# Cross attention of the last two sequences, started four rounds later

## What is computed

```python
x = _layernorm(x + _L0_attn_ref(...))
x = _layernorm(x + _L0_xattn_ref(...))
x = _layernorm(x + _L0_ffn_ref(...))
x = _layernorm(x + _L1_attn_ref(...))    # stage D: linear attention, 16 heads, causal
x = _layernorm(x + _L1_xattn_ref(...))   # stage E: cross attention, 16 heads, softmax
x = _layernorm(x + _L1_ffn_ref(...))     # stage F: 8 experts, the best two of each token
```

```python
attn = einsum('bhqd,bhkd->bhqk', q, k) * scale
attn = softmax(clip(attn, -CLAMP, CLAMP))
x = einsum('bhqk,bhkd->bqhd', attn, v).reshape(B, Nq, Cq) @ Wo + bo
```

## Time and profile before

| | |
|---|---|
| median of 3 runs | 1518.58 us (1508.76 to 1525.29) |
| profiled execution | 1518.51 us, its span 1516.7 us |
| PE, DVE, ACT, POOL busy | 1328.6, 908.3, 575.2, 801.0 us |
| mean granted clock of PE | 0.924 |
| PE waits of scores for the queries' load, 1018 to 1130 us | 19.4 us, 2 times |
| DVE busy, 1059.3 to 1080.2 and 1080.2 to 1109.7 us | 16.00 and 16.85 us |
| first expert block's transposes on PE | from 1198.51 us |

### The profile page before, as it was taken

The page is one execution under the profiler, slowest core; times in us unless marked ns, Lnnn a source line. Parts: engine busy times, 40 slices in busy tenths (PEclk is TensorE's granted clock), DMA queues, the critical chain, the costliest instruction groups (busy, mean ns, idle before and its releaser), DMA issues.

```text
span 1516.7 us, 23092 instructions
## 1 busy us (share of the span) xinstructions
PE 1328.6 (88%) x9071; PEld 1131.0 (75%) x9071; DVE 908.3 (60%) x1729; ACT 575.2 (38%) x1171; POOL 801.0 (53%) x762
## 2 busy tenths in 40 slices
PE   6996999999999999978898988986865399999990
PEld 6995788888888888855576666765754399999990
DVE  4666522732442452234577777786774499999986
ACT  3566211211111121023244444443432377777752
POOL 4433666666666576323123334334533678888742
PEclk9997899999999999988799999998776599999995
DMA  5100333333233233112233124224210666656615
GB/s 172 38 17 6 101 97 118 97 98 97 83 103 95 81 111 97 35 51 55 75 117 112 44 94 112 49 88 124 84 35 15 227 229 237 222 216 226 218 60 166
DMA packets 58044, 163.23 MB, mean 108 GB/s; under 512 B 10598, under 2 KB 26185, under 8 KB 50000
## 3 DMA queue, kind: packets, MB, share of 16 engines
q1 hardware_dynamic: 45760, 100.13, 22.4%
q0 software_dynamic: 12176, 61.63, 11.4%
HBM read 136.47 MB, written 27.08 MB: 108 GB/s over the span
## 4 chain that ended last, share of the span: by engine, by line
PE 70%; DVE 14%; DMA 5%; ACT 4%; issue 3%; SPq 2%; POOL 1%; another core or an unknown queue 0%; ACTq 0%; POOLq 0%; DVEq 0%
PE bank L386 16%; PE bank L388 15%; PE bank L387 15%; PE bank L1214 8%; PE bank L394 5%; PE bank L975 3%; PE bank L1056 2%; DVE topE L1717 2%; DVE shiftE L1726 2%; SPq L715 2%; DMA split_qk<-qk_lo 2%; DMA xt_hi<-split_qk 1%; PE bank L1132 1%; PE bank L1043 1%; ACT x_tok L434 1%
## 5 line engine op out<-in xcount | busy, mean ns | idle before, releaser
L1590 DVE CAST hid_hi<-bank 128x512 fp32r<-128x512 f32 x96 | 66.4, 692 | 252.0 <-ACT bank L1329 250.9
L518 POOL TENSOR_TENSOR wpiece_lo<-wraw,wpiece_hi 128x1024 fp32r<-128x1024 f32 x88 | 210.9, 2397 | 7.4
L387 PE MATMUL bank<-hid_lo,wpiece_hi 128*128 128x512 f32 x512 | 199.4, 390 | 0.0
L386 PE MATMUL bank<-hid_hi,wpiece_lo 128*128 128x512 f32 x512 | 199.4, 389 | 0.0
L388 PE MATMUL bank<-hid_hi,wpiece_hi 128*128 128x512 f32 x512 | 199.4, 389 | 0.0
L516 POOL TENSOR_SCALAR wpiece_hi<-wraw 128x1024 fp32r<-128x1024 f32 x88 | 93.9, 1067 | 157.4 <-PE bank L388 129.5
L1329 ACT ACTIVATE bank<-bank,ffn_scales 128x512 f32<-128x512 f32 x64 | 42.4, 662 | 301.5 <-PE bank L388 301.5
L634 POOL TENSOR_SCALAR staging<-staging 128x1024 f32<-128x1024 f32 x64 | 66.6, 1041 | 134.3 <-ACT staging L1414 134.0
L1414 ACT ACTIVATE staging<-bank 128x512 f32<-128x512 f32 x128 | 70.0, 596 | 119.7 <-PE bank L1132 77.2
L386 PEld LDWEIGHTS bank<-hid_hi,wpiece_lo 128*128 128x128 f32 x512 | 96.2, 188 | 20.1
L388 PEld LDWEIGHTS bank<-hid_hi,wpiece_hi 128*128 128x128 f32 x512 | 96.1, 188 | 20.0
(11 more groups left out here) (337 smaller groups left out, 3752.2 us busy)
## 6 DMA issues: line engine op xcount, KB each, us to landing
wraw<-in_C_w SPq DMA_DIRECT2D x88, 512.0 KB, 3.6
split_qk<-qk_hi SPq DMA_DIRECT2D x64, 128.0 KB, 2.4
split_qk<-qk_lo SPq DMA_DIRECT2D x64, 128.0 KB, 2.4
xt_lo<-split_qk SPq DMA_DIRECT2D x8, 1024.0 KB, 5.7
xt_hi<-split_qk SPq DMA_DIRECT2D x8, 1024.0 KB, 5.8
yc<-y_rows SPq DMA_DIRECT2D x16, 256.0 KB, 5.8
ctx_raw<-in_ctxT SPq DMA_DIRECT2D x16, 192.0 KB, 4.0
xraw<-in_xT SPq DMA_DIRECT2D x8, 256.0 KB, 3.8
```

What stands on the lines that cost most here:

```text
L386: pe.e.matmul(o, sl, mh, start=start and i == 0, stop=False)
L387: pe.e.matmul(o, sh, ml, start=False, stop=False)
L518: pool.e.tensor_tensor(pair[1], raw, f(pair[0]), ALU.subtract).then_inc(done, 1)
```

## The change

For the last two sequences e becomes d + 22, so their PAIR, EDR and EFIN steps stand four rounds later; EPRE, which was written from e, is written from d and stays where it was.

```diff
         d = 4 + PAIRS * b
-        e = d + 18
+        e = d + (18 if b < B - 2 else 22)
...
-        items.append((e - 6, 5, "EPRE", (b,), (0, 1, 2, 7)))
+        items.append((d + 12, 5, "EPRE", (b,), (0, 1, 2, 7)))
         items += [(e + p, (0, 1, 2), "PAIR", (b, p), (0, 2, 4)) for p in range(PAIRS)]
         items += [(e + 8 + 4 * c, 5, "EDR", (b, c), 1) for c in range(KC)]
         items.append((e + 13, 5, "EFIN", (b,), (0, 1, 2, 4, 4, 5, 7, 8)))
```

## The result

The changed kernel took 1504.76 us (median of 19 runs, 1495.25 to 1519.68), the kernel before 1519.49 us beside it (19 runs): a ratio of 0.9928, 95% interval 0.9907 to 0.995. That is 7.6 to 14.1 us less, about 10.9; 13.5 were forecast. The ratio is not the quotient of the two medians, which lie 14.7 us apart (0.9903, a little outside the interval). So the runs show a gain, but not whether it is 10.9 us or the forecast 13.5. The profiled execution took 1496.94 us, its span was 1495.1.

A forecast was written before the change was run, and what follows sets the result against it. At the attention stage's end PE waits 19.4 us for the DMA of rearranged queries; then DVE is the limit. Eighth's PAIR 0 12.2 us earlier plus 1.3 at the end: 13.5 us, 1518.5 to 1505.0 us; range 1498 to 1515.

The forecast's parts named there:

- Step 1: First wait, 10.57 us: the eighth's close starts at once and takes 11.7 us, so its key product comes 12.3 us earlier.
- Step 2: Second wait, 8.86 us: from the eighth's key product to its queries landing is a 32.25 us chain, independent of pairs.
- Step 3: Seventh's PAIR 0 to eighth's: DVE has 28.4 us of work, filling the second wait; eighth's PAIR 0 12.2 us earlier.
- hold-up: Seventh's first pair: transposes wait for the bank ACT frees by copying the eighth's queries; 1.2 us, between 0 and 3.3.
- Step 4: Eighth's PAIR 0 to the last pair's end: 1.3 us saved (0 to 2.6), as the eighth's values come earlier.
- A: Close stays at 14.8 us and the bank hold-up costs its full 3.3: 7.1 us gained, 1511.4 us; chance 0.15.
- B: Close as short as the bare one, nothing holds DVE up: 17 us gained, 1501.6 us; chance 0.12.
- C: PE stays at 1.2 GHz in thin rounds 70 to 73, the close's products 2.7 us later: 1507.7 us; chance 0.13.
- D: Slower: seventh's pairs go at the hand-overs' pace, 5.2 us each (slower from 4.85): 1521.3 us; chance 0.06.
- E: PE waits for something else at the two places, so the change does nothing: 1518.5 us; chance 0.02.

## Why the prediction was right, and where it was off

The time and the chain of steps held; by the ratio and by the two profiles the gain was some 3 us smaller than the sum, and the interval holds the sum too. From the anchor, step by step, one execution against one:

Step 1, the close, held: 11.55 us against 11.7, and the key product 12.5 us earlier against 12.3. POOL's split of the context ended at 1053.63 (1052.37 + 1.26), 0.3 us ahead of the key product, where 0.4 was forecast. The closeness is partly luck, since the same instructions took 12.53 and 13.32 us in the two kernels with a shortened clamp.

Step 2, the chain of the eighth's queries: nothing waits at its PAIR 0, 34.2 us behind the key product (1088.15 - 1053.97), so 32.25 is not contradicted; the moment of landing has no row. The load was issued 25.6 us behind the key product (1079.52), 23.7 before. If it took 8.0 to 8.6 us as in the kernel before, an estimate, it landed at 1087.5 to 1088.1, just ahead of PAIR 0: the second wait was gone with little to spare.

Step 3 is the term that was mis-sized. Until DVE took up the seventh's PAIR 0 it was 3.67 us, as forecast (3.6). From there to the eighth's PAIR 0 it took 31.81 us where 28.4 of work and 1.2 of hold-up had been put; DVE was busy for 29.61. So the work was 1.2 us larger and the idle time 2.2 instead of 1.2. The work: a pair's price of 2.6 us came from rows in which the clamp ran at its short duration. Here two of the eight clamps (0.96 and 0.69 us instead of 0.16), the operation on `slot` (1.23 instead of 0.16) and the one on `lnE_rstd` (1.08 instead of 0.17) stood beside POOL and took 3.3 us more than at their short durations; the stretch of before that the sum started from holds 1.2 us of this kind. The idle time: the hold-up that step 3 named does not show, since DVE worked without a pause worth naming from 1057.64 to 1070.78, past the copy of the queries that ends at 1066.2. It stood still for 0.56 us ahead of the residual at 1071.33 and 0.55 ahead of the values at 1083.11, and the rest are pauses of at most 0.13 us. PE's 3.17 us of waiting for `shiftE`, the second entry of its waits, are PE waiting for DVE and no hold-up of DVE. P7 came 10.1 us earlier instead of 12.2.

Step 4: 1.8 us from P7 to the last pair's end (30.05 against 31.83), 1.3 forecast. Behind the last pair 1.3 us were lost (375.60 against 374.34), where nothing was forecast; that is less than two executions differ by. Sum: 10.1 + 1.8 - 1.3 = 10.6.

The rivals: A asked for a close of 14.8 us and B for nothing held up, neither came. C did not: the two products of the close ran with a granted clock of 1.00, that is 2.4 GHz, and only the key product, behind 2.79 us of waiting for `x_tok`, at 0.54, near 1.2 GHz, as before the change (0.52 from 1077.45 to 1080.18). D put pairs at 4.85 us or more; the seventh's took 4.0 each (31.81 / 8). No rival named what the moved scatters showed: with the queries in time, the version with the pairs beside the close was 6.7 us faster than the one with them behind it. E is excluded by the two waits that are gone.

What the prediction did not see is where the waits came from. It took the landing of the queries as given ("whatever PE does") and read the chain of 32.25 us as one of stores and loads. The rows of SP, which it did not use, show 5 to 6 us between last store and load that no store explains. For this change that made no difference to the sum. For the choice of a change it makes all the difference: moving four small DMAs removes most of the cause and leaves the pairs where they fill the close.

No version here is shown to be the best: two rounds later (0.9895), the change (0.9928) and the scatters alone (0.9929) lie within each other's intervals. The two kernels with a shortened clamp do not compute the same thing.

## What to carry to other kernels

When an engine waits for a transfer, first read the queue that issued it: the gap between the last store and the load that depends on it, against the same gap elsewhere in the kernel, says whether the trip is long or delayed by a neighbour. Moving the consumer back gains only as long as the delay is there and cost 6.7 us here once it was gone. Where DVE sets the pace, a per-tile price read where POOL was idle during its short operations is too low where POOL is busy.

## What the runs showed of the hardware

Four small indirect DMAs of POOL delay SP's transfers by far more than their bytes: they are 128 packets, 0.3% of the DMA engines' time between 1030 and 1062 us of the kernel before, and from last store to load it was 7.8 us with them and 2.5 with them moved. Busy times of the kernel before, microsecond by microsecond of the gap between last store and load (last columns: DMA share, GB/s):

```profile
1046.00:1047.00 1.00, 1.00 (x12) 0.86 (x8) 0.96 (x3) 0.00 (x0) 0.95 (x1) 1.00 0.07 9
1047.00:1048.00 1.00, 1.00 (x18) 0.42 (x16) 0.93 (x4) 0.00 (x0) 0.69 (x2) 1.00 0.03 1
...
1050.00:1051.00 1.00, 0.00 (x0) 0.00 (x0) 0.96 (x2) 0.00 (x0) 1.00 (x2) 1.00 0.00 0
```

The DMA engines were nearly idle while SP still waited for the stores to be reported as landed, until 1051.29. The Trainium skill, DMA: Bandwidth & Descriptors (SWDGE vs HWDGE vs iDMA), says that transfers issued by GpSimd and by SyncE feed different queues inside each DMA engine, which serves them in turn; taken alone, that rule would let the scatters cost the stores no more than their own share, and it does not explain the trace, in which the engines were nearly idle for some 5 us. Which part holds the report back stays open. It need not be the same for a load: in the kernel with keys and context early, whose load was issued beside the scatters and took 14.0 us, the engines were busy (share 1.05) from 1049 to 1054 us and moved 87 GB/s.

A DVE operation of 128x4 elements whose two inputs both lie in SBUF takes 0.16 us alone and up to 1.02 beside a POOL operation of 1.04, and short again when that is cut. The operations on the 1024 scores, with one input in a bank, kept 1.21 to 1.23 us. The Trainium skill, SBUF — State Buffer (SBUF: two separate sides), says that a VectorE operation with two SBUF inputs and a GpSimd operation that reads SBUF take a shared port by turns, each for its whole length; here the trace agrees. That sentence does not cover the operation on `lnE_rstd`, 128x2 with one input, which was stretched as well, to 1.08 us beside POOL's clamp and 0.18 when that was cut.
